# State product one step behind the closing of a batch, and the token chain one step later, in a fused attention and expert layer

## The reference, cut to what matters

```python
q, k, v = split(x @ Wq.T + bq), split(x @ Wk.T + bk), split(x @ Wv.T + bv)
q = softmax(q, axis=-1)          # over the 16 channels of a head
k = softmax(k, axis=-2)          # over the 1024 tokens of a batch
state = einsum('bhnd,bhne->bhde', k, v)
out = einsum('bhnd,bhde->bhne', q, state)
x = layernorm(x + layernorm_affine(out) @ Wo.T + bo)
x = layernorm(x + cross_attention(ctx, x, mask))
w, e = top_k(softmax(x @ router), 4); w = w / sum(w)
x = layernorm(x + sum_k w_k * (gelu(x @ up[e_k]) @ down[e_k]))
```

## Time and profile before

| | |
|---|---|
| median of the runs | 1258.03 us |
| the profiled execution | 1262.06 us, its span 1260.1 us |
| mean granted TensorE clock | 0.938 of full |
| busy: PE / PEld / DVE / ACT / POOL | 86 / 72 / 61 / 39 / 51% |
| DMA | 105.07 MB, mean 83 GB/s |
| first expert product | 427.54 us from the start |

### The profile page before, as it was taken

How to read it: one execution, slowest core, us unless ns; L and a number is a source line. 1 busy time by engine, 2 the same in 40 slices (tenths; PEclk the granted TensorE clock), 3 DMA queues, 4 the chain that set the end, 5 groups by cost and what they waited for, 6 DMA issues and landing times.

```text
span 1260.1 us, 27063 instructions
## 1 busy us (share of the span) xinstructions
PE 1086.4 (86%) x8572; PEld 908.3 (72%) x8572; DVE 764.3 (61%) x1863; ACT 495.3 (39%) x913; POOL 647.3 (51%) x738
## 2 busy tenths in 40 slices
PE   6668877878886699988899999999999999999960
PEld 3345665656565588877788888888888888888750
DVE  1667988977797687765744444444444444444325
ACT  3754533544353255543233333333333333333214
POOL 3013327745673777766775465555555555554424
PEclk9779989988897799999999999999999999999995
DMA  5431223222212233334444654465544445553325
GB/s 163 150 105 60 93 85 93 77 78 63 76 38 64 67 60 74 73 63 75 60 72 79 131 89 78 77 77 77 77 77 77 77 77 77 77 77 60 65 55 242
DMA packets 163039, 105.07 MB, mean 83 GB/s; under 512 B 107596, under 2 KB 153856, under 8 KB 162656
## 3 DMA queue, kind: packets, MB, share of 16 engines
q1 hardware_dynamic: 132896, 67.67, 21.2%
q0 software_dynamic: 30016, 35.68, 19.7%
HBM read 51.91 MB, written 36.04 MB: 70 GB/s over the span
## 4 chain that ended last, share of the span: by engine, by line
PE 59%; DVE 17%; POOL 11%; issue 6%; ACT 3%; DMA 3%; SPq 0%; POOLq 0%; DVEq 0%; ACTq 0%
PE big L1665 25%; PE big L1684 13%; PE trans L1684 12%; POOL slot_records L781 3%; POOL rstd L757 3%; PE big L1707 2%; DVE stat L1049 2%; PE small L1753 2%; POOL early_sums L811 2%; POOL ve L755 1%; DVE w_up L1045 1%; PE small L1585 1%; PE big L1709 1%; DVE w_down L1045 1%; DVE pr L1334 1%
## 5 line engine op out<-in xcount | busy, mean ns | idle before, releaser
L1665 PE MATMUL big<-xgT,w_up 128*128 128x256 f16 (+1 forms) x3456 | 408.5, 267 | 14.4 <-DMA xgT<-xg 11.7
L1665 PEld LDWEIGHTS big<-xgT,w_up 128*128 x3456 | 325.3, 98 | 57.8 <-issue 18.3
L904 ACT ACTIVATE h<-big,up_scale 128x512 f32<-128x512 f32 x270 | 185.5, 687 | 449.9 <-PE big L1665 436.8
L1298 DVE TENSOR_SCALAR hh<-h,h_scale 128x512 f16<-128x512 f32 x270 | 133.5, 494 | 314.0 <-ACT h L904 312.2
L811 POOL DMA_INDIRECT token_sums<-y,rec x99 | 164.2, 1659 | 243.0 <-ACT y L912 205.9
L1684 PE MATMUL big<-w_down,hh 128*128 x1264 | 217.8, 274 | 2.7 <-DVE hl L1300 2.4
L1300 DVE SCALAR_TENSOR_TENSOR hl<-h,h_scale,hh 128x512 f16<-128x512 f32 x270 | 203.0, 752 | 9.6
L1684 PE MATMUL big<-w_down,hl 128*128 x632 | 173.4, 274 | 0.0
L1684 PE MATMUL trans<-w_down,hh 128*128 x896 | 153.4, 273 | 2.5 <-DVE hl L1300 2.4
L781 POOL DMA_INDIRECT slot_records<-recs,posi x128 | 130.0, 1015 | 35.6 <-issue 33.6
L1684 PEld LDWEIGHTS big<-w_down,hh 128*128 128x128 f16 x1264 | 124.2, 98 | 21.5 <-issue 5.2
(11 more groups left out here) (251 smaller groups left out, 1511.9 us busy)
## 6 DMA issues: line engine op xcount, KB each, us to landing
w_down<-in_L_ffn_up_w_dram SPq DMA_DIRECT2D x8, 1024.0 KB, 5.1
w_down<-in_L_ffn_down_w_dram SPq DMA_DIRECT2D x7, 1024.0 KB, 6.0
XA<-in_x_dram SPq DMA_DIRECT2D x32, 128.0 KB, 2.8
XRES<-in_x_dram SPq DMA_DIRECT2D x32, 128.0 KB, 2.6
token_rows<-XR SPq DMA_DIRECT2D x32, 128.0 KB, 1.9
sums<-token_sums SPq DMA_DIRECT2D x8, 512.0 KB, 6.5
out_dram<-sums SPq DMA_DIRECT2D x8, 512.0 KB, 2.6
xgT<-xg SPq DMA_TRANSPOSE x135
```

The lines of the kernel that those rows point to most:

```text
L904: act.activation(h[:, i % H_RING, :], psu[up_bank(i)], ACT.Gelu_apprx_tanh, scale=k["up_scale"][:, t:t + 1]).then_inc(gelu_ready, 1)
L1298: dve.tensor_scalar(hh[:, i % HALF_RING, :], h[:, i % H_RING, :], k["h_scale"][:, t:t + 1], None, ALU.mult).then_inc(hh_ready, 1)
L1665: ins = pe.matmul(psu[up_bank(i)][:, j * size(t):(j + 1) * size(t)], w[:, ws, c, m:m + P], xgT[:, t % 2, xs * CC + c, 0:size(t)], start=(n ...
```

## The change

The state product and `build_state` of a batch move from its closing step to the end of the next step. The lowering of the keys stays in the closing step, at its very end on DVE (`lower_keys`, five pieces instead of four), and ACT takes the exponentials in the next step, behind the query exponential and ahead of a weight piece's split and the probability copies. The chain runs one step later (`s - (TB + 2) - d`), and so there are 50 steps instead of 49 and 12 mixed steps instead of 11, MIX0 staying 38. Since the next batch's first two tiles arrive before the state product, K, V have a spare place (over the last expert's up weights) and Q nine places. The turn of the context keys and `key_blocks` move from the head of a step to its end. `choose` moves by two steps for the first half of a batch and by one for the second. The weight pieces come in steps 11, 13, 15, 19, 23, 28, 32, 35 instead of 12, 15, 18, 21, 24, 28, 32, 36, the last one staged over the projection's weights and inputs. The twelve loads of context values come a step later. The early tiles read and add to the same HBM tensors as the others, so the copies of rows, slot records and sums go; there are 19 early tiles instead of 18.

```diff
-CONST_STEPS = 31 + 3 * FCH + TOPK + EXP
+CONST_STEPS = 32 + 3 * FCH + TOPK + EXP
-PIECE_STEPS = [2, 3, 4, 5, 6, 7, 8, 9, 12, 15, 18, 21, 24, 28, 32, 36]
-HALF_STEPS = [TB + 4 + HT * (half + 1) for half in range(HALVES)]
+PIECE_STEPS = [2, 3, 4, 5, 6, 7, 8, 9, 11, 13, 15, 19, 23, 28, 32, 35]
+HALF_STEPS = [2 * TB + 2, 2 * TB + 5]
-EARLY = 18
+EARLY = 19
-MIX0 = PIECE_STEPS[-1] + 2
+MIX0 = PIECE_STEPS[-1] + 3
 def chain_tile(s, d):
-    return first_tile(s - (TB + 1) - d)
+    return first_tile(s - (TB + 2) - d)
+def state_built(s):
+    return closing(s - 1) if s >= 1 else None
+EXTRA = TB
+HOME = [[0, 1], [EXTRA, 1], [0, EXTRA], [1, 0]]
+def home(g):
+    b, i = divmod(g, TB)
+    return HOME[b][i] if i < 2 else i
+def home_before(g):
+    return max((u // TB for u in range(g) if home(u) == home(g)), default=None)
+KEY_GROUPS = [(0, 1), (1, 2), (2, 4), (4, 6), (6, 8)]
...
# SP
                 elif n == 2 * EXP - 1:
-                    sp.wait_ge(sm_ready, SM["st", B - 1, CC - 1] + 1)
+                    sp.wait_ge(big_ready, BIG["qkv", NT - 1] + 1)
...
-                sp.dma_start((acc1_out if g < EARLY_TILES else acc_out)[g], X2[:, g % 3, :]).then_inc(acc_stored[g % 3], 16)
+                sp.dma_start(acc_out[g], X2[:, g % 3, :]).then_inc(acc_stored[g % 3], 16)
...
-                if g < EARLY_TILES:
-                    sp.dma_start(rows1_out[g], XR[:, g % 2, :].bitcast(F32)).then_inc(rows_stored[g % 2], 16)
...
                     sp.wait_ge(early_step, EARLY_SLOTS)
-                    sp.wait_ge(records_copied, 16 * EXP)
+                    for half in range(HALVES):
+                        sp.wait_ge(scattered[half], 16 * HT * TOPK * EARLY_BATCHES)
...
-                if i == 2 and 0 <= b < B:
+                if i == 3 and 0 <= b < B:
                     load_values(b)
...
-                if s == record_step(EARLY_BATCHES) - 1:
-                    for half in range(HALVES):
-                        sp.wait_ge(scattered[half], 16 * HT * TOPK * EARLY_BATCHES)
-                    for e in range(EXP):
-                        at = slice(e * CAP, e * CAP + EARLY_BATCHES * N)
-                        sp.dma_start(slots1[at, :], slots[at, :]).then_inc(records_copied, 16)
...
-                if t == EARLY + 2:
-                    for u in (EARLY - 2, EARLY - 1):
-                        sp.wait_ge(y_added[u % 2], moved(u))
-                    for g in range(EARLY_TILES):
-                        sp.dma_start(acc_out[g], acc1_out[g]).then_inc(sums_copied, 16)
# POOL
-                b, i = divmod(s - TB - 1, TB + 1)
+                b, i = divmod(s - TB - 2, TB + 1)
                 if i == 0 and 0 <= b < B:
                     mask_row(b)
# ACT
-                    if a >= TB:
-                        act.wait_ge(sm_ready, SM["st", a // TB - 1, CC - 1] + 1)
+                    if home_before(a) is not None:
+                        act.wait_ge(sm_ready, SM["st", home_before(a), CC - 1] + 1)
...
                     act.wait_ge(qs_ready, a + 1)
-                    act.activation(Q[:, a % TB, :], Q[:, a % TB, :], ACT.Exp).then_inc(qe_ready, 1)
+                    act.activation(query_tile(a), query_tile(a), ACT.Exp).then_inc(qe_ready, 1)
+                b = state_built(s)
+                if b is not None:
+                    for q in range(len(KEY_GROUPS)):
+                        act.wait_ge(ks_ready, len(KEY_GROUPS) * b + q + 1)
+                        act.activation(key_group(b, q), key_group(b, q), ACT.Exp).then_inc(ke_ready, 1)
                 if split_piece(s) is not None:
                     split_high(split_piece(s))
                 if c3 is not None:
                     copy_probs("pa", c3)
                     copy_probs("pb", c3)
-                b = closing(s)
-                if b is not None:
-                    for q in range(KG):
...
# DVE
-                b, i = divmod(s - TB - 2, TB + 1)
-                if i == 0 and 0 <= b < B:
-                    key_blocks(b)
...
-                if close is not None:
-                    build_state(close)
+                if state_built(s) is not None:
+                    build_state(state_built(s))
...
                 if c3 is not None:
                     second_sum(c3)
+                b, i = divmod(s - TB - 2, TB + 1)
+                if i == 0 and 0 <= b < B:
+                    key_blocks(b)
+                if close is not None:
+                    lower_keys(close)
# PE
                 if c4 is not None:
                     turn_second(c4)
                     route(c4)
-                if close is not None:
-                    pe.wait_ge(kv_ready, 2 * TB * (close + 1))
...
+                last = state_built(s)
+                if last is not None:
+                    pe.wait_ge(kv_ready, 2 * TB * (last + 1))
+                    for c in range(CC):
+                        dst = small_into(("st", last, c))
+                        for q, (i0, i1) in enumerate(KEY_GROUPS):
+                            if c == 0:
+                                pe.wait_ge(ke_ready, len(KEY_GROUPS) * last + q + 1)
+                            for i in range(i0, i1):
...
                 positions(s)
+                b, i = divmod(s - TB - 2, TB + 1)
+                if i == 0 and 0 <= b < B:
+                    pe.wait_ge(ctx_loaded, 16 * (b + 1))
+                    for c in range(CC):
+                        pe.transpose(small_into(("kt", b, c))[:, 0:KEYS], ctx_sb[:, c * P:(c + 1) * P], ident[0:KEYS, 0:KEYS]).then_inc(sm_ready, 1)
```

99 lines of the change are left out of this document (46 added, 53 removed).

## The result

The changed kernel takes 1273.33 us (median of four runs, 1271.52 to 1275.69) against 1258.68 for the kernel before: ratio 1.0118, 95% interval 1.0096 to 1.014, so 14.7 us slower. The forecast was 1256.5 us with a range of 1246 to 1265. The profiled execution took 1274.66 us, 12.60 more than that of the kernel before.

The account below looks back on a forecast made before the run. DVE was taken to set the pace to about 427 us, then PE and POOL, then PE alone. From 1262.06, first regime -7.3 and mixed regime +5.8 gave 1260.6, less 4.0: 1256.5 us; 8 in 10 for 1246 to 1265.

Parts of the forecast that it names:

- POOL's scatters: Mixed steps: the two eight-scatter steps, now separated from the fullest chain, lose a PE pause; -6.5 us, between 0 and -10.
- The closings: Batches 1 and 2: exponentials ahead of probability copies add 1.5 us of waiting, the first sum 0.4; +3.8 us in all.
- The granted clock: Ordinary steps: the closing step loses its long PE pause, so the clock gains slightly; -1.0 us, bounds -9 and +9.
- the clock turns against it: Rival, first regime: PE idles more often in short pieces, 9 us more, 1265.5; chance 0.17 shared with SP's wait near its upper bound.
- Batch 0: First closing, no chain yet: the serial stretch overlaps the next step's projection, mostly refilled by ACT and lowering; -1.5 us, 0 to -5.0.
- One chain tile fewer: Before the seam: DVE has done one tile's chain less by step 34; -7.3 us, all on DVE.
- The state wait only moves: Behind closings: DVE's 5.0 us of waiting for the state product stays, a step later, because its bank order is unchanged.
- The seam: Step 34's last router copy to first expert product: step 37 starts 5.5 us later, gathers save 6.8; -1.3 us.
- SP's new wait: Mixed step 38: twelve context-value loads ahead of the transposes delay PE 5.5 us, plus 1.3 for the clock; +6.8 us.
- The copies: Copies of slot records and early sums and second row stores removed: no effect on time, 0 us.
- the extra step: Mixed regime: one more full mixed step (16.0 us) in place of a bare tile (10.5); +5.5 us.

Follow-up runs that it names:

- the best: Changed kernel with context values loaded later, key exponentials behind probabilities in batches 1 to 3, scatters spread, state read late: 1245.62 us (5 runs) and 1247.37 us (8 runs).

## Why the prediction was wrong

Two steps of it failed: the cost of the exponentials' place together with the clock, and the relief of POOL's scatters. Against the profiled execution the sum was 1260.6 and the time 1274.66, 14.1 more: 8.3 in the first regime and 6.0 behind the first expert product, less 0.2 by which the time grew less than the span. The median of before lies 4.0 under its profiled run, that of the changed kernel 1.3, which is the rest of the 16.8 us to 1256.5.

*The closings (+3.8, of which 3.0 for the exponentials): the first step that failed.* The mechanism was named and its size was wrong. The sum took the delay of ACT's copies less the slack ahead of DVE's first use, 1.5 us a closing. In batch 1 the order cost 5.1 us from closing to closing: 2.4 of it is the wait for the value shares itself, 2.8 are waits for projections in ordinary steps, for which the sum had no term (smaller ones cancel). In batch 2 it cost 1.7 (111.7 against 110.0). With the order changed in batches 1 to 3 alone, 7.5 us of the time went. With that edit the first expert product stands at 421.65, 1.4 from the forecast's 420.2. With it the changed kernel is still slower than the kernel before (ratio 1.0053), so this step alone doesn't turn the sign. Against the kernel before the loss sits mostly in batch 1: DVE's idle time there grew by 7.9 us, in batch 2 by 0.6, since the same waits for the value shares come in it but those for the projection fell from 10.3 to 5.9.

*The granted clock (-1.0, bounds -9 and +9).* The rival "the clock turns against it" had the right sign and, in batch 1, the right place, and was too short by itself: it gave 1265.5. From closing to closing batch 1 had 0.97 before and 0.89 in two profiles after, batch 2 0.87 and then 0.88 in both. The sentence that spoke against the rival, that PE gains work in the closings, didn't hold it off. What makes the level fall isn't settled: more PE work in the ordinary steps left the time as it was, and a PE pause of 1.23 in place of 3.40 left the fall in step 18 where it was. The Trainium skill (TensorE: Matmul & The Clock Gate, section "HAM oscillation — how this bites in real kernels") has a case where waits between groups of matmuls bring the lower clock back each time. The trace agrees in that the 0.50 stands behind PE's waits in step 18 of all three profiles shown; it doesn't bear out that the length of one wait decides, with 3.40, 2.83 and 1.23 us ahead of the same fall.

*Batch 0 (-1.5, bounds 0 and -5.0).* From closing to closing DVE's idle time was 21.3 us before and 24.0 and 21.5 in two profiles after, so +0.2 to +2.7. The closing itself lost 4.1 us of DVE's idle time; but the state's wait moved to step 9 and stayed (5.8), and the waits for the query projections grew by 1.0. Taking the state's wait away uncovered ACT. What failed here is "overlaps the next step's projection": the exponentials, the piece and the product were still one behind the other.

*One chain tile fewer (-7.3).* DVE's busy time up to the first expert product fell by 6.2. Right within 1.1.

*The state wait only moves.* Right: 5.0 before, 5.9 after, and for the reason given. What the prediction didn't see is that in the new step the routing choice follows it and can cover it, so that reading the state later removes most of the wait (5.9 to 1.1), though only 3.9 us of the time. In the kernel before the gates follow in that step, and their product stands behind the state's on PE, so there, by the code, the two would wait for each other; that wasn't run.

*The seam (-1.3).* From the last router copy of step 34 it took 52.6 us before and 49.6 after, -3.0. Step 37 started 2.9 us later against step 34, where 5.5 was forecast, and the first gather came 2.7 us into it, as forecast. The second gather took 0.98 us, with the low half of the last piece done before it (in rows 7 it took 2.83 beside it):

```profile
405.91 2.35 DVE L1064 SCALAR_TENSOR_TENSOR w_down<-wqkv_XA,wsc,w_down 128x2048 f16<-128x2048 f32 x1
...
418.62 1.11 POOL L816 DMA_INDIRECT xg<-token_rows,rec  x1 [0.32 <-issue]
420.04 0.98 POOL L816 DMA_INDIRECT xg<-token_rows,rec  x1 [0.30 <-issue]
```

It isn't chance: with the split beside it the second gather took 2.83, 2.84 and 2.89 us in the three kernels with the order of before, with the split done 0.95 to 0.99 in all fifteen profiles with the changed order. That is the -1.8 in the sum. It is also what the Trainium skill's rule of shared access (SBUF — State Buffer, section "SBUF: two separate sides") would give; the trace agrees in size, and no row shows the port's mode.

*SP's new wait (+6.8).* Right: 7.2 in the first mixed step, 6.3 to 6.5 given back when the loads move.

*POOL's scatters (-6.5, bounds 0 and -10): the second step that failed.* Of the 11.8 us behind the first expert product 5.5 were to come from the extra step and 7.2 are SP's, which leaves -0.9 for this term, near its bound of 0. It was said that a step without scatters would stand between the two with eight and the fullest chain. What sets the pause is the eight scatters in a row with two adds ahead of the deviation of a tile that PE is waiting for, and in the changed kernel one such step still has a chain tile in it. The pause was 4.88 where before had 3.56 and 2.98. Spreading them was worth 7.5 us, as the forecast had for the change, which doesn't do it.

*The copies (0).* On the kernel before they were worth about 2.4 us. That is to the change's credit, so the rest of it cost some 2 us more than the total shows.

## What to carry to other kernels

Of work put ahead of something that feeds TensorE, expect more than its delay: 2.4 us of exponentials ahead of the probability copies cost 7.5 us over three closings, where the delay less the slack came to 3 for two. How much of the rest is the clock's answer to the pause no run here separates, so try the order and don't price it. Before a wait is called moved and kept, look what stands behind it in its new step: reading a result behind independent work of the same engine can take the wait away, and the next engine in line (ACT here) decides what is left. Before an edit is credited to a new order, make it on the old one too: the spread scatters brought the kernel before to within 1 to 3 us of the best. A relief that hangs on where a queue's burst falls is only had by breaking the burst.

## What the runs showed of the hardware

- The 1.2 GHz level came back behind short pauses of PE: at 174.4 behind two of 1.23 and 1.19 us with the exponentials moved, at 174.4 behind one of 3.40 without. It held for 6.9 us in the first case and 10.2 in the second.
- With 4.1 us more PE work from closing to closing the granted clock was 0.91 (0.89 without) and the length the same.
- Two executions of the same program differ by 4.8 us at the first expert product (428.50 and 423.70), 1.7 of it ahead of the first closing and 2.6 in batch 0 with a clock of 0.85 or 0.91 there; the totals differ by 2.0. A single profile can't size a term of 2 us in this regime.
- An indirect DMA that POOL issues took about 1.0 us with 0.3 between two, in bursts of eight as in bursts of four; the adds took 1.8 each. The exception is the gather beside DVE's split of a weight piece, with 2.83 to 2.89.
